# Output projection of an attention block: three f32r passes over a split weight in place of plain fp32

## The reference

```python
x = x + tanh(g_xattn[0]) * xattn(layernorm(x), ctx, ctx, mask, w_q, b_q, ..., w_o, b_o)
x = x + tanh(g_ffn[0]) * ffn(layernorm(x), gate_w, eg, eu, ed, sg, su, sd)

# xattn: 16 heads of 16
scores = einsum('bhqd,bhkd->bhqk', qh, kh) * 16 ** -0.5
attn = softmax(where(mask == 0, -10000.0, scores))
out = einsum('bhqk,bhkd->bhqd', attn, vh).reshape(B, Sq, 256)
return out @ w_o + b_o
```

## Time and profile before

| | |
|---|---|
| median of 3 runs | 884.07 us (882.83 to 884.09) |
| the profiled execution | 881.68 us, its span 879.9 us |
| PE busy | 846.5 us, 96% of the span |
| DVE busy | 581.9 us, 66% |
| ACT busy | 520.8 us, 59% |
| GpSimd busy | 461.2 us, 52% |
| granted TensorE clock | 0.992 of full speed |

### The profile page before, as it was taken

The page is one execution under the profiler, slowest core; times in us unless marked ns, Lnnn a source line. Parts: engine busy times, 40 slices in busy tenths (PEclk is TensorE's granted clock), DMA queues, the critical chain, the costliest instruction groups (busy, mean ns, idle before and its releaser), DMA issues.

```text
span 879.9 us, 19161 instructions
## 1 busy us (share of the span) xinstructions
PE 846.5 (96%) x6271; PEld 742.7 (84%) x6272; DVE 581.9 (66%) x1203; ACT 520.8 (59%) x1846; POOL 461.2 (52%) x551
## 2 busy tenths in 40 slices
PE   8788999999999999999999999999999999999995
PEld 7566788888888799999988888888888888889994
DVE  6899899999998577876564555555555545444442
ACT  4999999999999444656464444444445444322221
POOL 6686767667565353676531454444443444364442
PEclk9899999999999999999999999999999999999998
DMA  7125233322313222333240333222222232232221
GB/s 219 42 77 180 68 90 94 90 66 90 90 66 96 73 74 85 120 103 103 86 141 25 49 49 49 43 41 38 41 41 42 47 48 37 31 49 42 36 40 20
DMA packets 56887, 62.05 MB, mean 71 GB/s; under 512 B 15642, under 2 KB 45183, under 8 KB 56799
## 3 DMA queue, kind: packets, MB, share of 16 engines
q1 hardware_dynamic: 42871, 43.15, 15.8%
q0 software_dynamic: 12864, 17.57, 12.7%
q10 hardware_dynamic: 1064, 0.21, 0.1%
HBM read 34.78 MB, written 25.82 MB: 69 GB/s over the span
## 4 chain that ended last, share of the span: by engine, by line
PE 85%; ACT 5%; DVE 5%; issue 2%; DMA 1%; POOL 1%; DVEq 0%; SPq 0%; ACTq 0%; POOLq 0%
PE p_s L623 23%; PE p_f L640 12%; PE p_f L2767 9%; PE p_s L341 6%; PE p_f L2812 5%; PE p_s L2767 4%; ACT prob L1484 4%; PE p_t L2698 3%; PE p_t L352 3%; PE p_s L2684 3%; PE p_m L2725 3%; PE p_m L2665 2%; PE p_m L2713 2%; PE p_s L2812 2%; PE p_s L2870 1%
## 5 line engine op out<-in xcount | busy, mean ns | idle before, releaser
L509 POOL DMA_INDIRECT out_rows<-big_yout,slot_id x52 | 86.6, 1666 | 158.2 <-DVE big_yout L586 146.3
L1484 ACT ACTIVATE prob<-p_s,negmax 128x77 f32<-128x77 f32 x512 | 161.1, 372 | 7.2 <-DVE negmax L2032 7.0
L537 ACT ACTIVATE big_sil<-p_s 128x512 f32<-128x512 f32 (+1 forms) x78 | 46.6, 597 | 144.7 <-PE p_s L623 126.1
L1484 ACT ACTIVATION_READ_ACCUMULATOR prob<-p_s,negmax 128x1 f32 x512 | 128.9, 255 | 0.0
L569 DVE TENSOR_TENSOR big_hid<-p_s,big_sil 128x512 f32<-128x512 f32 (+1 forms) x78 | 54.0, 692 | 99.5 <-ACT big_sil L537 88.5
L623 PE MATMUL p_s<-big_fxT_hi,big_w_hi 128*128 128x512 f32 (+1 forms) x286 | 113.8, 398 | 0.3 <-ACT big_w_hi L529 0.3
L623 PE MATMUL p_s<-big_fxT_lo,big_w_hi 128*128 128x512 f32 (+1 forms) x286 | 112.7, 394 | 0.0
L623 PE MATMUL p_s<-big_fxT_hi,big_w_lo 128*128 128x512 f32 (+1 forms) x286 | 112.2, 392 | 0.0
L1108 POOL TENSOR_TENSOR prob<-prob,rinv 128x616 f32<-128x616 f32 x64 | 78.5, 1236 | 62.1 <-DVE rinv L2039 62.1
L1127 POOL TENSOR_TENSOR shT_lo<-shid,shT_hi 128x256 fp32r<-128x256 f32 x80 | 63.0, 800 | 44.4 <-ACT shT_hi L1526 44.3
L640 PE MATMUL p_f<-wd_hi,big_hT_hi 128*128 (+1 forms) x312 | 85.5, 280 | 0.0
(11 more groups left out here) (341 smaller groups left out, 2537.7 us busy)
## 6 DMA issues: line engine op xcount, KB each, us to landing
xr<-in_x SPq DMA_DIRECT2D x16, 256.0 KB, 2.9
x_scratch<-xr SPq DMA_DIRECT2D x16, 256.0 KB, 2.8
xn_scratch<-xn SPq DMA_DIRECT2D x16, 256.0 KB, 2.1
xt_scratch<-xnT SPq DMA_DIRECT2D x16, 256.0 KB, 3.2
xin<-xt_scratch SPq DMA_DIRECT2D x16, 256.0 KB, 3.6
x1in<-x_scratch SPq DMA_DIRECT2D x16, 256.0 KB, 3.3
out_rows<-syout SPq DMA_DIRECT2D x16, 256.0 KB, 2.2
raw<-in_L_ffn_ed SPq DMA_DIRECT2D x4, 688.0 KB, 4.3
```

Of the source, the lines that this page charges most:

```text
L509: pool.indirect_dma_start(out, bass.IndirectOffsetOnAxis(slot_id[:, column(j, t)], 0), yout[:, t, :], None, compute_op=ALU.add).then_inc(s ...
L1484: last = act.activation(prob[n % 2][t][:, m * PW + h * SK:m * PW + (h + 1) * SK], p_s[:, 2 * t + h // 4, col:col + SK], ACT.Exp, bias=negm ...
```

## The change

The weight `w_o` is loaded into `wo_in`. GpSimd splits it once, in `split_wo`, into `wo_hi` (f32r) and `wo_lo`, which lies where `wo_in` lay. DVE's `attention_out` writes `oT_hi` as f32r and, in one more instruction, `oT_lo = p_m - oT_hi`, which waits for the first; `oT_lo` lies where `kT` lay, no longer needed by then. PE's `out_proj` waits for s_oTlo and runs three passes: 12 f32r matmuls of 128 x 256 instead of 4 in fp32.

```diff
@@ memory
+        wo_at = home.at
+        wo_in = sb("wo_in", [P, KC, H])
+        wo_lo = Home(nc, wo_at, home.at).sb("wo_lo", [P, KC, H], f32r)
...
-        wo = sb("wo", [P, KC, H])
+        wo_hi = sb("wo_hi", [P, KC, H], f32r)
+        kT_at = home.at
         kT = sb("kT", [P, KC, B * SK])
+        oT_lo = Home(nc, kT_at, home.at).sb("oT_lo", [P, KC, UT * P], f32r)
...
-        oT = sb("oT", [P, KC, UT * P])
+        oT_hi = sb("oT_hi", [P, KC, UT * P], f32r)
@@ GpSimd
+            def split_wo():
+                pool.wait_ge(s_wo, 16)
+                pool.tensor_copy(wo_hi[:, :, :], wo_in[:, :, :]).then_inc(s_wosplit, 1)
+                pool.wait_ge(s_wosplit, 1)
+                pool.tensor_tensor(wo_lo[:, :, :], wo_in[:, :, :], wo_hi[:, :, :], ALU.subtract).then_inc(s_wosplit, 1)
...
                 normalise(0, 2)
+                split_wo()
                 normalise(0, 3)
@@ VectorE
             def attention_out(n):
                 dve.wait_ge(s_PV, n + 1)
                 wait(dve, s_Wo, n)
-                nc.vector.tensor_copy(oT[:, :, :], cols(p_m[:, :])).then_inc(s_oT, 1)
+                nc.vector.tensor_copy(oT_hi[:, :, :], cols(p_m[:, :])).then_inc(s_oT, 1)
+                dve.wait_ge(s_oT, n + 1)
+                nc.vector.tensor_tensor(oT_lo[:, :, :], cols(p_m[:, :]), oT_hi[:, :, :], ALU.subtract).then_inc(s_oTlo, 1)
@@ TensorE
             def out_proj(n):
-                pe.wait_ge(s_oT, n + 1)
                 if n == 0:
-                    pe.wait_ge(s_wo, 16)
+                    pe.wait_ge(s_wosplit, 2)
+                pe.wait_ge(s_oTlo, n + 1)
                 for t in range(UT):
-                    for m in range(KC):
-                        last = nc.tensor.matmul(p_m[:, t * H:(t + 1) * H], oT[:, m, t * P:(t + 1) * P], wo[:, m, :],
-                                                start=(m == 0), stop=(m == KC - 1))
+                    for q, (o, w) in enumerate(PASSES):
+                        for m in range(KC):
+                            last = nc.tensor.matmul(p_m[:, t * H:(t + 1) * H],
+                                                    (oT_lo if o else oT_hi)[:, m, t * P:(t + 1) * P],
+                                                    (wo_lo if w else wo_hi)[:, m, :],
+                                                    start=(q == 0 and m == 0), stop=(q == 2 and m == KC - 1))
                 last.then_inc(s_Wo, 1)
```

More of the change, by code:

```diff
@@ L672, in attend_share_route @@
         ewgu, ewd = v["wgu"], v["wd"]
-        sb = Home(nc, AT[0], AT[0] + 3 * GU1).sb
+        home = Home(nc, AT[0], AT[0] + 3 * GU1)
+        sb = home.sb
         kblk = [sb(f"kblk_{s}", [P, 2, KC * HW], f32r) for s in ("hi", "lo")]
@@ L687, in attend_share_route @@
         xnT = sb("xnT", [P, 2, KC, UT * P])
-        sb = Home(nc, AT[3], AT[3] + 2 * WD1).sb
+        home = Home(nc, AT[3], AT[3] + 2 * WD1)
+        sb = home.sb
         vall = sb("vall", [SK, B, H])
         wq = sb("wq", [P, KC, H])
-        wo = sb("wo", [P, KC, H])
+        wo_hi = sb("wo_hi", [P, KC, H], f32r)
+        kT_at = home.at
         kT = sb("kT", [P, KC, B * SK])
+        oT_lo = Home(nc, kT_at, home.at).sb("oT_lo", [P, KC, UT * P], f32r)
         mask_in = sb("mask_in", [P, 2, UT, SK], i32)
@@ L789, in attend_share_route @@
         p_f = [ps(f"p_f{k}", [P, 512]) for k in range(2)]
+        s_wosplit, s_oTlo = sem("s_wosplit"), sem("s_oTlo")
         s_ctx, s_wk, s_wv, s_wq, s_wo, s_gw, s_bias, s_tgb, s_init = (sem(n) for n in (
@@ L1006, in _ @@
                 sp.dma_start(raw[k][0:FT, (FC - 1) * H:FC * H], src[full:FF, :]).then_inc(s_sraw[kind], 16)
-            sp.dma_start(wo[:, :, :], v["w_o"].rearrange("(c p) d -> p c d", p=P)).then_inc(s_wo, 16)
+            sp.dma_start(wo_in[:, :, :], v["w_o"].rearrange("(c p) d -> p c d", p=P)).then_inc(s_wo, 16)
             for n in range(2, XR):
```

## The result

The changed kernel takes 888.68 us (median of 5 runs, 887.49 to 889.34), the kernel before 883.22 on the same chip (5 runs): ratio 1.0056, 95% interval 1.0042 to 1.0071. By the medians it is 5.5 us slower, by the ratio 4.9 (3.7 to 6.3). The granted clock was 0.99 in both. The time lies inside the forecast of 886 to 892.

The account below looks back on a forecast made before the run. PE is nearly full, but DVE's `attended` sets when it starts `x_T` in even steps. Terms 3.1 + 1.0 + 0.6 + 0.4 + 0.1 = +5.2, taken as +4.5: 884.07 + 4.5 = 888.6 us; range 881.5 to 893, D's own 886 to 892.

Parts of the forecast that it names:

- PE's saving: At the output projection: twelve f32r matmuls, 1.41 us, save 0.41 in even steps and 0.32 in odd, mostly lost in waits.
- The idleness before `x_T`: PE's idle time before the transposes into p_m in even steps: to grow from 0.34 to about 1 us.
- DVE's instruction: The subtraction `oT_lo` ahead of `attended`: 0.73 us a unit with its wait, bounds 0.68 and 0.78, 11.7 us in all.
- The dearer bound: `oT_lo` held up like the slowest `xn`: 0.75 us more a unit, 12 us in all; not added.
- first four units: First four steps, lower half of 0 to 2 x 0.73: +0.4 us; step at 75 us: another 0.4.
- even steps, units 4 to 12: Four tight steps where `x_T` waits for `attended`: 4 x 0.73 - 0.2 = 2.7 us; the step at 253 us gives nothing.
- odd steps, units 5 to 13: DVE 0.73 late, partly absorbed before `x_T`: 0.2 us in each of five steps, +1.0 us.
- units 14 and 15: PE already waits for `oT` at the output projection: 0.73 - 0.41 = 0.3 us each, +0.6 us.
- The split of the weight: On GpSimd, once, between unit 0's third and fourth normalise: at most 2.4 us in a gap of 2.29, +0.1 us.
- A: Rival: PE's saving comes through at the transposes behind `attended`; faster, 879, or 881 if half the steps stall; chance 0.15.
- B: Rival: even steps lose 0.3 to 0.4, odd ones gain as much; 884 with 1.8 to either side; chance 0.16.
- C: Rival: DVE bounds the whole stage; 11.7 us come through but for a quarter: +8 to +11.7, 892 to 896; chance 0.11.

Follow-up runs that it names:

- a kernel with the idleness before `x_T` removed: Second-layernorm statistics moved behind `attended`, on the changed kernel (890.45 us) and on the one before (888.60); statistics behind `q_lo` plus mask comparison later, on the changed kernel (894.60).
- the two with the mask comparison: DVE's mask comparison `no_sight(i+1)` moved behind `half_max(i, 3)` in even steps: on the changed kernel 887.10 us, on the kernel before 882.10 us.

## Why the prediction was right

- **What bounds the kernel.** Right: PE is the fullest engine, and yet its time is set by DVE at `x_T`. In the changed kernel the 0.10 us behind `attended` stand in the even steps of units 4 to 10, and now in the odd ones of units 5 to 11 too. The subtraction alone gives the whole loss.
- **PE's saving.** Mostly swallowed, as forecast. Its size was too large: to the next group 1.62 us in place of 1.82 in even steps and 1.51 in place of 1.73 in odd ones, where 1.41 was forecast. In odd steps, behind the fp32 transposes, the first pair takes 0.32 us where later ones take 0.24; for this stall the text allowed. Even steps have no fp32 work on either side, and lose 0.1 twice. The last pair takes 0.33 us to the start of the scores, and 0.32 in the kernel without the subtraction. The first takes 0.34, but only behind the wait: it takes 0.23 in that other kernel, where PE doesn't wait, and the fp32 projection that waits takes 0.1 longer as well (1.92). The saving was worth 1.2 us where DVE did nothing more.
- **The idleness before `x_T`.** Forecast to grow to about 1 us, and it is 0.56 to 0.94. PE waits 0.20 us at the projection, not 0.36, and saves less there. At 145 us DVE's stretch from copy to `attended` also grew by less than the 0.73 (from 3.72 to 4.08 us). From unit 3 to unit 12 a pair of steps is 0.6 us longer on average, at the low end of the 0.6 to 0.9, with single pairs from 0.3 to 1.1.
- **DVE's instruction.** 0.691 us in all 16 cases, with 0.03 us of wait for the cast (149.19 + 0.69 to 149.91): 0.72 against 0.73. The dearer bound, 1.4 us by the slowest `xn`, did not come true.
- **The projection waits for `oT_lo`.** In even steps it starts 0.06 us behind its end, as forecast. The prediction spoke of all twelve matmuls behind that wait, though only the third pass reads `oT_lo`. An earlier start of the first two passes wasn't tried: they write p_m, the bank which the subtraction is still reading.
- **The terms of the sum.** Two measures answer to them. One is the lateness that `attended` gains from unit to unit between the two profiled executions, less the 1.1 us of the start; the other is the kernels with the subtraction in some units only, their time shared out by the same reading of their traces.

| term | forecast | gained in the trace | by experiment |
|---|---|---|---|
| first four units | 0.4 + 0.4 | 1.9 | 1.0 (units 0 to 3) |
| even steps, units 4 to 12 | 2.7 | 2.1 | 3.3 of 4.1 (even units 4 to 14) |
| odd steps, units 5 to 13 | 1.0 | 0.4 | 0.4 of 1.0 (odd units 5 to 15) |
| units 14 and 15 | 0.6 | 0.8 | 0.8 + 0.8, without PE's saving |
| sum | 5.1 | 5.2 | 6.1 by the times |

  (The tenth that lacks to 5.2 in the forecast is the split.) That the even units carry the loss is right, and so is the full 0.7 us at the four tight ones. Two sizes were off and a third is open. The first four steps are the open one: "the lower half" of 0 to 2 x 0.73 was a choice without a row behind it. The trace has 0.9 us at unit 1 alone, where PE waits 0.34 us for `oT_lo`; its 0.5 at unit 0 is within what executions differ by at this place, so the 1.9 is uncertain by as much and more, and the experiment's 1.0 (0.1 to 1.8) doesn't differ from the forecast 0.8. Unit 12 was put at nothing and costs 0.3 to 0.5 where the even units stand alone. The odd steps were put at 1.0 and leave 0.4. These errors go both ways, and it is partly luck that the sum came out better than its parts.
- **The split of the weight.** Forecast +0.1, measured nothing. The two instructions take 1.03 and 1.28 us in the gap of the earlier trace rows, and the fourth `normalise` starts 1.08 us later, as does the whole program in that execution. On GpSimd:

```profile
30.14 1.03 POOL L1236 CAST wo_hi<-wo_in 128x512 fp32r<-128x512 f32 x1
31.25 1.28 POOL L1238 TENSOR_TENSOR wo_lo<-wo_in,wo_hi 128x512 fp32r<-128x512 f32 x1
32.49 1.22 POOL L1116 TENSOR_TENSOR prob<-prob,rinv 128x616 f32<-128x616 f32 x1
```

- **From the sum to the median.** The sum of 5.2 was cut to 4.5 for delays that might be absorbed. The stage shows 5.3 and the medians 5.5, on a median of before that was itself 0.9 us lower this time (883.22). The 888.6 was hit partly because these two offset each other.
- **The rivals.** A (PE's saving comes through) fell: the saving stands as idleness before `x_T`, and two passes in place of three change the time by 1 us. B, 884 with 1.8 to either side, fell with the interval of the ratio, whose lower end is +3.7 us. C (DVE bounds the whole stage, +8 to +11.7) fell with the +5.5, and with the kernels that gave DVE time back behind `x_T`, 1 us a pair of steps, and gained 0.8 us by the ratios.

What did not hold are the ideas formed after the result. Three times a kernel with the idleness before `x_T` removed was expected to be faster, and three times it was slower, by 3 to 7 us by the ratios over its starting point. The cast on ScalarE and the two with the mask comparison missed their forecasts as well. None of the reorderings won back the loss. The lowest time of one that computes the reference is 882.10, the kernel before with the mask comparison moved, and its interval reaches 1.0000. Whether another order of the steps can hold the f32r projection at no cost stays open.

## What to carry to other kernels

Price a new instruction by the release point ahead of which it stands, not by its engine's busy share: here 0.69 us on an engine 90% busy cost all of itself in the four units where a 99% busy PE stood 0.1 us behind it and in the last two, where PE stood waiting for its result, and on average 0.1 us in the odd units between. Work taken off the fullest engine is worth nothing at a place where it waits at the next hand-over anyway; look for the first instruction behind the saving that starts on another engine's signal. In an order balanced over three engines, removing one wait by moving work moves the wait; trace what the moved instruction is now ahead of, down to the third engine, before counting a gain.

## What the runs showed of the hardware

- An f32r matmul of 128x256 starts every 0.117 us with its weight load hidden, an fp32 one of that shape every 0.43 (1.73 us for four). Three passes are 81% of the fp32 time. With stalls of 0.1 us, one behind fp32 transposes in odd steps, two at a wait and at the scores in even ones, 87 to 89% was reached.
- DVE instructions of one size stretch or not by where their inputs lie. `oT_lo`, with an input in PSUM, took 0.691 us in 16 of 16 cases, but the mask comparison of 154 elements anything from 0.19 to 1.26, and a pair of `xn` 0.83 or 1.79, the long ones shown here beside a GpSimd instruction, which itself grew from 1.22 to 1.46 or 1.35. The Trainium skill ("SBUF — State Buffer", section "Who interferes with whom") says that DVE contends with GpSimd when it has two SBUF inputs or runs in a two-port mode, which one-input operations like `tensor_scalar` can enter, and not otherwise. These rows agree; that the comparison ran in such a mode no row shows. A moved instruction can therefore change its own length, as `xn` did.
- In the 14 profiled executions PE's first large group starts between 9.99 and 11.12 us, in 12 of them at the landing of `wq`, though nothing ahead of it was changed. That is more than half of the 1.8 us that this measurement can tell from no change. Two traces are compared after taking out this difference, and even then the first 48 us leave up to 2.6 us open.
